# Five of sixteen products per unit on TensorE, and another order of the last steps, in a Mamba and attention/MoE kernel

## The chip, the cores and the metric

One NeuronCore of one Trainium2 chip runs the whole program. The metric is the time of the program on the device in microseconds (us), as the median of several runs.

## The reference, cut to what matters

The input x is 8 sequences of 512 tokens with 128 channels, in float32. Layer one is a Mamba block that runs over each sequence forward and backward, layer two is attention with a mixture of experts. What matters of the first is this:

```python
dt = softplus(dtr @ Wdt.T + bdt)                    # (tokens, 256)
h  = exp(dt_t[..., None] * A) * h + (dt_t * u_t)[..., None] * B_t[:, None, :]   # 16 states for each of 256 channels
y_t = einsum('bdn,bn->bd', h, C_t)
```

The end of layer two adds the two chosen experts' rows of every token to x2, normalizes the sum over its channels, and adds x:

```python
out = out + einsum('tf,hf->th', g, w2[e]) * wfull[:, e:e+1]   # for each expert e
x = x + layernorm(x2 + out)
```

## The kernel before, in words

The first phase (`mamba_phase`) goes through 16 units: for each of the 8 sequences b a forward one (d = 0) and a backward one (d = 1). A unit is 32 steps s, for state n = s // 2 and channel half h = s % 2. Time runs along the free axis (512), channels lie on the partitions. For each step

- ScalarE makes `da` = exp(dt * A) (line 622), up to 8 steps ahead of the scan (`NDA`);
- dt\*u\*B is made in one of two ways. For 12 of the 16 states TensorE spreads B over the partitions into a bank of `bp` (`pe_b`, line 398, one bf16 matmul), and VectorE multiplies by `dtu` into a bank of `dbu` (`dve_dbu`, line 729). For the 4 states in `BY_PE` TensorE makes the whole product, as a matmul of the transposed dt\*u with a diagonal matrix that holds B (`pe_fill`, line 373, four float32 matmuls for each half). The diagonals are made by ScalarE (`act_diag`, line 590, four instructions a state), at the steps in `DIAG_AT`, in two buffers in turn;
- VectorE runs the scan (`dve_scan`, line 745), GpSimd multiplies by C (`pool_hc`, line 874), and TensorE transposes and sums into `yp` (`pe_y`, line 410).

Each engine's order is written out by hand. In `pe_unit` the first fill of a state n is issued at step 2n - 1 and the second at step 2n + 2. Into the same in-order queue go the matmuls that prepare the next unit (`front`): `pe_u` at steps 12 to 18, `pe_z` at 19 and 20 (they wait for ScalarE's silu of u, line 542, which stands behind `da` of step 25), `pe_xd` at 21 (line 339), and `pe_dt` at 24 and 25 (line 389). The previous unit's output (`tail`) is transposed at step 7, copied by ScalarE at its steps 14 and 15 (`act_ygt`, line 630), and, in forward units alone, multiplied by Wout at steps 10 to 13 (`pe_out`, line 432). On VectorE, `dve_dt` makes dt and dtu of the next unit at steps 29 and 30 (lines 715 and 720).

The second phase (`ffn_phase`) runs over slots, 40 for a sequence. A table of due slots (`PLAN`, and `last_plan` for the last three sequences) says at which slot each engine issues a step. At the end of a sequence, SyncE stores the experts' rows (`sp_y`, line 1383), loads x2 again (`sp_x2e`, line 1313, which waits until VectorE has read the former one), and loads x (`sp_xr`); GpSimd gathers each token's two rows (line 2242); VectorE adds them (`ye`, line 2071), takes the statistics (lines 1856 and 1860); and GpSimd normalizes and adds (`pool_rstd`, `pool_out`, lines 2209, 2212 and 2216), and SyncE stores (line 1387). In a slot of SyncE x2e stands ahead of y. VectorE's first `ye` of a sequence waits until `pool_out` of the sequence before is through, because it writes the same tile `ye`.

Of the kernel before, what the change touches and what calls it, by code (L numbers as in the profile page):

```python
# [18 lines left out]
ALU = mybir.AluOpType  # L19
ACT = mybir.ActivationFunctionType  # L20
# [5 lines left out]
P = 128  # L26
NB = 8
# [47 lines left out]
    return isinstance(b, int) and b == 0  # L75


BY_PE = ((2, 4, 12, 14), (2, 4, 6, 14))
N_PE = len(BY_PE[0])
DIAG_AT = ((-1, 5, 18, 20), (-1, 5, 11, 20))  # L80


def made_by_pe(d, n):
# [17 lines left out]
def mamba_phase(nc, sems, x, x1, cscr, w):  # L101

    with ExitStack() as ctx:
# [258 lines left out]
        def pe_fill(pe, b, d, n, h):  # L362

            e = BY_PE[d].index(n)
            if h == 0:
                pe.wait_ge(diag_done, count(diag_done, b, TC * (N_PE * d + e + 1)))
                pe.wait_ge(dtt_done, count(dtt_done, b, 2 * d + 2))
                pe_bank_free(pe, b, d, n)
            else:
                pe.wait_ge(scan_done, count(scan_done, b, STEPS * d + 2 * n - 1))  # L370
            dst = dbu[:, dbu_bank(d, n), :] if h else bp[:, n % 2, :]
            for c in range(TC):
                last = nc.tensor.matmul(dst[:, c * P:(c + 1) * P], dtt[:, c, h * P:(h + 1) * P], diag[:, e % 2, c, :],  # L373
                                        start=True, stop=True)
            last.then_inc(fill_done if h else b_ready, 1)

# [208 lines left out]
        def act_diag(act, b, d, e):  # L585

            act.wait_ge(bt_done, count(bt_done, b, d + 1))
            act.wait_ge(fill_done, count(fill_done, b, N_PE * d + e - 1))
            for c in range(TC):
                nc.scalar.activation(diag[:, e % 2, c, :], ident[:, :], ACT.Copy,  # L590
                                     scale=bt[:, d, c, BY_PE[d][e]:BY_PE[d][e] + 1]).then_inc(diag_done, 1)

        def act_soft(act, b, d, h, k):
# [392 lines left out]
def last_plan(f):  # L986

    if f == NB - 3:
        at = PLAN["down"], PLAN["y_copy"]
        return {"down": at[0][:-1] + (125,), "y_copy": at[1][:-1] + (126,), "y": (99, 109, 119, 126),  # L990
                "gather": (132, 132, 133, 133, 134, 134, 135, 135), "ye": (141, 142),
                "end": (143, 144), "end_rstd": 144, "yo": (144, 145, 146), "out": 147}
    if f == NB - 2:
        return dict(in_pairs(88), w=(73, 80, 80, 97), rows=79, y=(100, 101, 110, 111), x2e=110, xr=110,
                    gather=(114, 114, 115, 115, 116, 116, 117, 117), ye=(129, 130), end=(130, 131), end_rstd=136,
                    yo=(136, 137, 138), out=139)
    if f == NB - 1:
        return dict(in_pairs(68), og_fin=(43, 44, 45, 46), wo=47, post=(48, 49, 49), x2=48, rms=50, h2n=51, x2t=52, h2t=52,
                    gate=54, ex=55, count=57, gate_step=(55,) * 5 + (56,) * 4 + (57,) * 6 + (58,) * 5 + (59,) * 3 + (60,) * 4,
                    scatter=(59, 60, 60, 61, 61, 62, 62, 63), rows=64, w=(61, 62, 69, 70), keep=62, y=(80, 81, 90, 91),  # L1000
                    x2e=91, xr=99, gather=(92, 92, 93, 93, 94, 94, 95, 95), ye=(97, 98), end=(99, 99), end_rstd=100,
                    yo=(100, 101, 102), out=103)
    return {}

# [70 lines left out]
def ffn_phase(nc, sems, x1, out, qscr, kscr, xs, ys, h0s, x2s, w):  # L1075

    with ExitStack() as ctx:
# [776 lines left out]
        def dve_stats(side, src, sem):  # L1854
            for c in range(TC):
                nc.vector.bn_stats(stats[:, side, c, :], src[:, c, :]).then_inc(sem, 1)
# [189 lines left out]
        def dve_g(dve, b, q, f):  # L2046
# [4 lines left out]
            if paired(b):  # L2051
# [5 lines left out]
            nc.vector.scalar_tensor_tensor(g[:, n % 2, 0:w_], ga[:, n % 2, 0:w_], 0.5, bank_of(b, q)[:, 0:w_],  # L2057
                                           ALU.mult, ALU.mult).then_inc(g_done, 1)

        def dve_end(dve, b, k, j=0):  # L2060
            if k == 0:
                if j == 0:
                    dve.wait_ge(gathered, count(gathered, b, 16 * TC * TOP))
                    dve.wait_ge(keep_done, count(keep_done, b, 2))
                    dve.wait_ge(out_done, count(out_done, b, 0))
                    dve.wait_ge(x2e_loaded, count(x2e_loaded, b, 16))
                    dve.wait_ge(end_step, count(end_step, b, 0))
                for c in range(TC):
                    if j:
                        dve.wait_ge(ye_done, count(ye_done, b, c + 1))  # L2070
                    nc.vector.scalar_tensor_tensor(ye[:, c, :], yk[:, c, j, :], wn_e[:, b % 2, c, j:j + 1],  # L2071
                                                   ye[:, c, :] if j else x2e[:, c, :],
                                                   ALU.mult, ALU.add).then_inc(ye_done, 1)
            elif k == 1:
                dve.wait_ge(ye_done, count(ye_done, b, 2 * TC))
                dve_stats(2, ye, end_step)
            else:
                dve_aggr(2, end_step)

        def dve_moe(dve, b, k):  # L2080
# [121 lines left out]
        def pool_out(pool, b, k):  # L2202
# [3 lines left out]
            if k == 0:  # L2206
                pool.wait_ge(end_rstd, count(end_rstd, b, 2))
                pool.wait_ge(out_stored, count(out_stored, b, 0))
                nc.gpsimd.tensor_tensor(yo[:, :, :], ye[:, :, :], mean, ALU.subtract).then_inc(out_done, 1)
            elif k == 1:  # L2210
                pool.wait_ge(out_done, count(out_done, b, 1))
                nc.gpsimd.tensor_tensor(yo[:, :, :], yo[:, :, :], r, ALU.mult).then_inc(out_done, 1)
# [197 lines left out]
```

## Time and profile before

Three runs took 1774.48, 1781.57 and 1783.27 us: a median of 1781.57 us. The profiled execution took 1780.3 us, and its span is 1778.6 us. The first phase ends near 1000 us.

| engine | busy us | share of the span |
|---|---|---|
| VectorE (DVE) | 1386.0 | 78% |
| TensorE (PE) | 1351.9 | 76% |
| GpSimd (POOL) | 1109.5 | 62% |
| ScalarE (ACT) | 1063.5 | 60% |

A share of busy time is a mean over the two phases. The row of busy tenths in 40 slices shows VectorE at nine tenths or more in every slice of the first phase after its start, and at four to eight tenths in most of the second. The granted TensorE clock is 0.88 of full speed over the span.

### The profile page before, as it was taken

What the parts mean: (1) busy time and instruction counts of PE and PEld (TensorE: products, weight loads), DVE (VectorE), ACT (ScalarE), POOL (GpSimd) and SP (SyncE); (2) the same over time, 40 slices, a digit from 0 to 9 for tenths busy, and PEclk for the clock granted to TensorE, in tenths of its full rate; (3) what the DMA queues carried; (4) which work ended last, traced back from release to release, by engine and by line L of the source; (5) the groups of instructions that cost most, each with busy time, mean ns of one, the idle gap of its engine ahead of it and who ended that gap; (6) DMA issues with size and microseconds to landing.
All of it is one profiled execution on the core that took longest, in us unless ns stands there. A gap on an engine that the chain in (4) does not pass through costs nothing. (4 is left out here: it accounts for less than half of the span.)

```text
span 1778.6 us, 30876 instructions
## 1 busy us (share of the span) xinstructions
PE 1351.9 (76%) x8880; PEld 980.9 (55%) x8880; DVE 1386.0 (78%) x2234; ACT 1063.5 (60%) x1888; POOL 1109.5 (62%) x1244
## 2 busy tenths in 40 slices
PE   3877787678777877887786427888989889888671
PEld 1566566556655665666565413335665566656571
DVE  1999999999899999999999416677678777777422
ACT  4777677776776776867766023655555555556330
POOL 1677777777777777877777423445456466555535
PEclk9898999898899898998897658888899998999886
DMA  4122302320223023202220111134556455454662
GB/s 133 55 101 96 120 1 95 119 95 18 102 95 119 1 95 119 95 17 103 95 95 19 31 51 46 44 97 130 164 170 200 143 170 159 131 186 153 216 209 69
DMA packets 114410, 184.90 MB, mean 104 GB/s; under 512 B 10384, under 2 KB 87184, under 8 KB 109968
## 3 DMA queue, kind: packets, MB, share of 16 engines
q1 hardware_dynamic: 110192, 175.15, 28.7%
q0 software_dynamic: 4096, 8.40, 1.6%
q8 instruction: 44, 0.72, 0.2%
q14 instruction: 78, 0.64, 0.1%
HBM read 153.03 MB, written 25.89 MB: 101 GB/s over the span
## 5 line engine op out<-in xcount | busy, mean ns | idle before, releaser
L874 POOL TENSOR_TENSOR hc<-hb,cb 128x512 f32<-128x512 f32 x512 | 653.6, 1296 | 208.4 <-DVE hb L745 178.1
L745 DVE TENSOR_TENSOR_SCAN hb<-da,dbu 128x512 f32<-128x512 f32 x448 | 527.7, 1205 | 19.0 <-PE dbu L373 13.3
L622 ACT ACTIVATE da<-dt,a_neg 128x512 f32<-128x512 f32 x512 | 351.7, 716 | 188.9 <-DVE hb L745 160.5
L410 PE MATMUL yp<-ident,hc 128*128 128x128 f32 x2048 | 327.0, 295 | 3.2 <-POOL hc L874 3.1
L410 PEld LDWEIGHTS yp<-ident,hc 128*128 128x128 f32 x2048 | 278.0, 155 | 83.0 <-issue 54.9
L1764 ACT ACTIVATE pt<-scores,lift 128x512 f32<-128x512 f32 x320 | 216.4, 684 | 169.7 <-PE scores L1515 161.9
L1891 DVE TENSOR_REDUCE mx<-ms 128x1 f32<-128x384 f32 (+3 forms) x352 | 218.3, 636 | 117.7 <-PE ms L1477 111.2
L729 DVE TENSOR_TENSOR dbu<-dtu,bp 128x512 f32<-128x512 f32 x384 | 251.3, 684 | 16.5 <-PE bp L398 7.3
L2222 POOL TENSOR_SCALAR_AFFINE_SELECT pt<-pt 128x256 f32<-128x256 f32 (+1 forms) x320 | 119.0, 375 | 199.0 <-ACT pt L1764 197.0
L321 PE MATMUL wp<-xpad,wu 128*128 128x512 f32 x256 | 132.1, 608 | 11.4 <-DVE res L760 6.5
L1477 PE MATMUL ms<-k,q 72*128 72x384 bf16 (+3 forms) x512 | 136.8, 326 | 0.0
L1515 PE MATMUL scores<-q,k 75*128 75x384 bf16 (+3 forms) x512 | 131.2, 319 | 2.2 <-ACT pt L1764 2.1
L1474 PE MATMUL ms<-mask,identb 128*128 128x128 bf16 (+2 forms) x352 | 92.2, 262 | 52.9 <-DVE mx L1891 23.1
L1534 PE MATMUL og<-pt,vpad 128*32 128x512 f32 (+3 forms) x1024 | 98.8, 484 | 23.4 <-POOL pt L2222 23.2
L2242 POOL DMA_INDIRECT yk<-ys_scratch,pos_e x64 | 61.6, 962 | 50.7 <-DMA ys_scratch<-ysb 35.8
L359 PE MATMUL wp<-ident,dtu 128*128 128x128 f32 x128 | 31.5, 427 | 80.0 <-DVE dtu L720 80.0
L398 PE MATMUL bp<-st,sel 96*128 96x512 bf16 x192 | 79.5, 414 | 11.9 <-DVE dbu L729 9.3
L1515 PEld LDWEIGHTS scores<-q,k 75*128 75x128 bf16 x512 | 48.9, 103 | 64.6 <-issue 34.6
L1474 PEld LDWEIGHTS ms<-mask,identb 128*128 128x128 bf16 x352 | 36.2, 103 | 87.5 <-issue 42.9
L373 PE MATMUL dbu<-diag,dtt 128*128 128x128 f32 x512 | 70.9, 282 | 15.6 <-DVE hb L745 15.1
L590 ACT ACTIVATE diag<-ident,bt 128x128 f32<-128x128 f32 x256 | 81.2, 389 | 1.6
L373 PEld LDWEIGHTS dbu<-diag,dtt 128*128 128x128 f32 x512 | 63.8, 192 | 31.6 <-DVE hb L745 24.9
(228 smaller groups left out, 2441.7 us busy)
## 6 DMA issues: line engine op xcount, KB each, us to landing
cb<-c_scratch SPq DMA_DIRECT2D x16, 3072.0 KB, 11.6
wt<-ffn_w_e SPq DMA_DIRECT2D x120, 384.0 KB, 4.3
cb<-c_scratch SPq DMA_DIRECT2D x16, 1024.0 KB, 4.5
q<-q_scratch SPq DMA_DIRECT2D x96, 96.0 KB
xg<-xs_scratch SPq DMA_DIRECT2D x24, 256.0 KB, 3.4
ys_scratch<-ysb SPq DMA_DIRECT2D x24, 256.0 KB
q_scratch<-qp SPq DMA_DIRECT2D x24, 128.0 KB
k<-k_scratch SPq DMA_DIRECT2D x32, 72.0 KB
```

What stands on the lines that cost most here:

```text
L321: last = nc.tensor.matmul(wp[:, h, :], wu[:, d, j, h * P:(h + 1) * P], xpad[:, d, j:j + SEQ], start=(j == 0), stop=(j == NTAP - 1))
L373: last = nc.tensor.matmul(dst[:, c * P:(c + 1) * P], dtt[:, c, h * P:(h + 1) * P], diag[:, e % 2, c, :], start=True, stop=True)
L410: last = nc.tensor.matmul(yp[:, c, h * P:(h + 1) * P], src[:, c * P:(c + 1) * P], ident[:, :], is_transpose=True, start=(s < 0 and h == 0 ...
L622: nc.scalar.activation(da[:, s % NDA, :], dt[:, h, :], ACT.Exp, scale=a_neg[:, d, h, n:n + 1]).then_inc(da_done, 1)
L729: nc.vector.tensor_tensor(dbu[:, dbu_bank(d, n) ^ h, :], dtu[:, h, :], bp[:, n % 2, :], ALU.mult).then_inc(dbu_done, 1)
L745: nc.vector.tensor_tensor_scan(hb[:, s % NHB, :], da[:, s % NDA, :], src, 0.0, ALU.mult, ALU.add).then_inc(scan_done, 1)
L874: nc.gpsimd.tensor_tensor(hc[:, s % NHC, :], hb[:, s % NHB, :], cb[:, d, s // 2, :], ALU.mult).then_inc(hc_done, 1)
L1474: nc.tensor.matmul(heads[:, :, c * P:width], identb[:, :], mask[:, :].unsqueeze(1).to_broadcast([P, n, P]), start=True, stop=False, skip_g ...
L1477: last = nc.tensor.matmul(heads[:, i, :], q9[0:PART_ROWS, at, h0_ % GH + i, c * P:(c + 1) * P], k9[0:PART_ROWS, at, 0:width], start=False, ...
L1515: last = nc.tensor.matmul(sp_[:, t % 2, at:at + SEQ - kc * P], k9[:, group, kc * P:(kc + 1) * P], q9[:, group, h % GH, kc * P:], start=Tru ...
L1764: nc.scalar.activation(pt[:, (ST_TILES * b + t) % NPR, 0:width], scores_in, ACT.Exp, bias=lift[:, :], scale=SCALE).then_inc(exp_done, 1)
L1891: nc.vector.reduce_max(mx[:, c, h:h + n], ms[:, t % 2, 0:n * (c + 1) * P].rearrange("p (n k) -> p n k", n=n), mybir.AxisListType.X).then_i ...
```

## The change

1. `BY_PE` has five states: (2, 4, 10, 12, 14) in forward units and (2, 4, 6, 12, 14) in backward ones. So state 10 is added in forward units and state 12 in backward ones, and their diagonals at ScalarE's steps 14 and 18; the forward unit's diagonal of state 14 moves from step 20 to step 28. With an odd number in a unit, the buffer of a diagonal goes by the count over both units.
2. In the last sequence, `x2e` is due one slot later (92, not 91), behind the last `y` of slot 91.
3. In the last sequence, `ye` is written into the tile `x2e` in place. The wait for GpSimd's `pool_out` of the sequence before goes from the first addition to the aggregation of the statistics, which writes the means that `pool_out` reads.

```diff
-BY_PE = ((2, 4, 12, 14), (2, 4, 6, 14))
+BY_PE = ((2, 4, 10, 12, 14), (2, 4, 6, 12, 14))
 N_PE = len(BY_PE[0])
-DIAG_AT = ((-1, 5, 18, 20), (-1, 5, 11, 20))
+DIAG_AT = ((-1, 5, 14, 18, 28), (-1, 5, 11, 18, 20))
...
-                last = nc.tensor.matmul(dst[:, c * P:(c + 1) * P], dtt[:, c, h * P:(h + 1) * P], diag[:, e % 2, c, :],
+                last = nc.tensor.matmul(dst[:, c * P:(c + 1) * P], dtt[:, c, h * P:(h + 1) * P], diag[:, (N_PE * d + e) % 2, c, :],
...
-                nc.scalar.activation(diag[:, e % 2, c, :], ident[:, :], ACT.Copy,
+                nc.scalar.activation(diag[:, (N_PE * d + e) % 2, c, :], ident[:, :], ACT.Copy,
...
-                    x2e=91, xr=99, gather=(92, 92, 93, 93, 94, 94, 95, 95), ye=(97, 98), end=(99, 99), end_rstd=100,
+                    x2e=92, xr=99, gather=(92, 92, 93, 93, 94, 94, 95, 95), ye=(97, 98), end=(99, 99), end_rstd=100,
...
+        def ye_of(b):
+
+            return x2e if b == NB - 1 else ye
+
...
-                    dve.wait_ge(out_done, count(out_done, b, 0))
+                    if b < NB - 1:
+                        dve.wait_ge(out_done, count(out_done, b, 0))
...
-                    nc.vector.scalar_tensor_tensor(ye[:, c, :], yk[:, c, j, :], wn_e[:, b % 2, c, j:j + 1],
-                                                   ye[:, c, :] if j else x2e[:, c, :],
+                    nc.vector.scalar_tensor_tensor(ye_of(b)[:, c, :], yk[:, c, j, :], wn_e[:, b % 2, c, j:j + 1],
+                                                   ye_of(b)[:, c, :] if j else x2e[:, c, :],
...
-                dve_stats(2, ye, end_step)
-            else:
+                dve_stats(2, ye_of(b), end_step)
+            else:
+                if b == NB - 1:
+                    dve.wait_ge(out_done, count(out_done, b, 0))
                 dve_aggr(2, end_step)
...
-                nc.gpsimd.tensor_tensor(yo[:, :, :], ye[:, :, :], mean, ALU.subtract).then_inc(out_done, 1)
+                nc.gpsimd.tensor_tensor(yo[:, :, :], ye_of(b)[:, :, :], mean, ALU.subtract).then_inc(out_done, 1)
```

## Rows read from the trace of the kernel before

**Rows 1.** Groups of instructions by line: busy us, mean ns, idle before.

```profile
L729 DVE TENSOR_TENSOR dbu<-dtu,bp 128x512 f32<-128x512 f32 x384 | 251.3, 684 | 16.5 <-PE bp L398 7.3 <-DVE hb L745 0.9
```

**Rows 2.** Busy time by stretch, two forward units, a backward unit, stretch after a wait.

```profile
283.20:343.00 59.80, 46.99 (x300) 36.86 (x299) 58.63 (x73) 41.39 (x75) 45.84 (x38) 0.93 0.23 89
402.60:464.40 61.80, 49.73 (x298) 38.81 (x297) 58.12 (x73) 41.28 (x74) 45.72 (x38) 0.89 0.22 86
...
464.40:522.20 57.80, 45.10 (x269) 35.10 (x268) 56.19 (x68) 45.57 (x84) 45.18 (x40) 0.91 0.18 73
...
436.50:444.50 8.00, 8.00 (x25) 5.76 (x26) 8.00 (x12) 4.42 (x7) 6.39 (x6) 0.62 0.29 98
```

**Rows 3.** VectorE in a forward unit by start time, and all instructions of L715.

```profile
318.95 1.26 DVE L729 TENSOR_TENSOR dbu<-dtu,bp 128x512 f32<-128x512 f32 x2
320.12 2.32 DVE L745 TENSOR_TENSOR_SCAN hb<-da,dbu 128x512 f32<-128x512 f32 x2
...
325.78 1.19 DVE L745 TENSOR_TENSOR_SCAN hb<-da,bp 128x512 f32<-128x512 f32 x1
...
331.78 1.19 DVE L745 TENSOR_TENSOR_SCAN hb<-da,bp 128x512 f32<-128x512 f32 x1
...
L715 DVE TENSOR_TENSOR dt<-t_ln,t_relu x16: 1224/1910/2589, 43.6 to 935.6; 128x1024 f32<-128x1024 f32 x16
```

**Rows 4.** TensorE in the same forward unit, by start time.

```profile
317.13 1.13 PE L330 MATMUL wp<-win_z,xpad 128*128 128x256 f32 x4 [2.81 <-ACT u L542]
...
321.78 0.60 PE L410 MATMUL yp<-ident,hc 128*128 128x128 f32 x4
322.21 1.06 PE L373 MATMUL bp<-diag,dtt 128*128 128x128 f32 x8
```

**Rows 5.** TensorE and VectorE in a backward unit, by start time.

```profile
504.66 1.12 PE L389 MATMUL wp<-xd,wdt 128*128 128x512 f32 x2 [0.39 <-ACT xd L563]
...
507.14 0.60 PE L410 MATMUL yp<-ident,hc 128*128 128x128 f32 x4
...
509.88 2.32 DVE L745 TENSOR_TENSOR_SCAN hb<-da,dbu 128x512 f32<-128x512 f32 x2
```

**Rows 6.** The same, in a backward and a forward unit with TensorE at half clock.

```profile
388.50 0.60 PE L410 MATMUL yp<-ident,hc 128*128 128x128 f32 x4
...
390.02 2.33 DVE L745 TENSOR_TENSOR_SCAN hb<-da,dbu 128x512 f32<-128x512 f32 x2
...
444.09 0.60 PE L410 MATMUL yp<-ident,hc 128*128 128x128 f32 x4
...
449.92 1.22 DVE L745 TENSOR_TENSOR_SCAN hb<-da,dbu 128x512 f32<-128x512 f32 x1 [1.65 <-PE dbu L373]
```

**Rows 7.** TensorE's first product with Wout, and ScalarE's diagonals, in a forward unit.

```profile
297.36 1.16 PE L432 MATMUL wp<-wout,ygt 128*128 128x128 f32 x8 [0.59 <-ACT ygt L630]
...
301.61 1.26 ACT L590 ACTIVATE diag<-ident,bt 128x128 f32<-128x128 f32 x4
```

**Rows 8.** The last 33 us by start time, and what SyncE waited for there.

```profile
1745.84 1.54 SPq L1383 DMA_DIRECT2D ys_scratch<-ysb  x3
1748.06 0.36 SPq L1313 DMA_DIRECT2D x2e<-x_scratch  x1
1748.52 0.54 SPq L1383 DMA_DIRECT2D ys_scratch<-ysb  x1
...
1752.56 0.94 POOL L2242 DMA_INDIRECT yk<-ys_scratch,pos_e  x1 [8.34 <-DMA ys_scratch<-ysb]
...
1765.91 1.26 POOL L2216 TENSOR_TENSOR yo<-yo,xr 128x512 f32<-128x512 f32 x1
...
1767.36 1.14 DVE L2071 SCALAR_TENSOR_TENSOR ye<-yk,wn_e,x2e 128x128 f32<-128x128 f32 x4 [18.05 <-POOL yo L2216]
...
1772.33 1.04 POOL L2209 TENSOR_TENSOR yo<-ye,mv 128x512 f32<-128x512 f32 x1
...
SPq L1077 <- DMA out<-yo: 1.9, 1, 1.9
```

## The prediction

> **What bounds the kernel now.** I read the busy tenths first, then the groups by line, then single units by their start times, and last the chain of waits at the end.
>
> In the first phase VectorE is the engine that never rests: in a forward unit of 59.8 us it is busy 58.6 us, TensorE 47.0, GpSimd 45.8, ScalarE 41.4 [rows 2]. The multiplication that the change takes away costs 684 ns each, and VectorE waited 16.5 us in all for what feeds it [rows 1]. So by shares VectorE is the bound, and one multiplication less should be one multiplication of time. But TensorE works through one hand-written order, and a share does not say whether a fill is ready when the scan asks for it. So the reader is to look at TensorE's start times beside VectorE's.
>
> Two things stand out. TensorE sits idle 2.81 us before the z matmuls of the next unit (it waits for ScalarE's silu), and from there on it works without a pause: z, y, xd, fills, dt [rows 4]. And forward units come in two lengths, 59.8 and 61.8 us [rows 2]: in the longer one that chain runs at a granted clock of 0.62, part of it at 1.2 and not at 2.4 GHz, and the scan waits 1.65 us for a fill [rows 2, 6]. I count this half clock behind the z wait in five of the eight forward units and in four of the seven backward units that prepare another; there the wait is 2.2 us.
>
> In the last 33 us the end is a chain over engines: store, gather, GpSimd's output of the sequence before, VectorE's additions, GpSimd's output, store [rows 8].
>
> **Part 1: the nominal gain.** Two multiplications go, a pair taking 1.17 us from start to next start (318.95 to 320.12). But the next state's multiplications then stand between the two scans. Four scans with one pair of multiplications took 5.66 us in one piece (320.12 to 325.78) and 6.00 us when interleaved (325.78 to 331.78), 0.34 more [rows 3]. So a state moved to TensorE gives 1.17 - 0.34 = 0.83 us, in 16 units 13.3 us, if its data are there in time.
>
> **Part 2: is the fill there in time, forward?** State 10's second fill is issued at step 22, which is just behind xd, where the y group starts at 321.78 now. A fill takes 1.06 us [rows 4], and I add 0.19 for the signal (the gap that I read wherever a scan waited for one): scan 21 can start at 323.03. Nominally it would start at 320.12 - 1.17 + 1.9 = 320.85, so it is 2.2 us late. Nothing upstream moves: the z wait ends 4.0 us after scan 17 starts, and scan 17 lies ahead of the change. Then come scan 21 with the multiplication behind it (1.85) and two scans (2.24): scan 24 starts at 327.12 instead of 325.78 [rows 3], +1.34. The second fill of state 12 is pushed back by the added 0.9 us and just makes it. Of the 1.34, dt gives back some: it took 2.59 us there, against a median of 1.91 [rows 3], because GpSimd was behind. That lag vanishes when the scans come later; I give back 0.7. A full-clock forward unit: +0.6 us, three of them +1.9.
>
> With the half clock: y behind xd starts at 444.09, so scan 21 at 445.34, scan 24 at 449.43, scan 25 at 451.33 instead of 449.92 [rows 6]: +1.4, five units +7.0.
>
> **Part 3: backward.** State 12's second fill is issued at step 26, behind both dt matmuls, where y starts at 507.14 now. Its first fill, at step 23, takes the place of a bf16 matmul and costs 0.67 more, of which TensorE's wait of 0.39 before dt hides its part: +0.28 [rows 5]. Scan 25 can start at 507.14 + 0.28 + 1.25 = 508.67, scan 26 at 510.52 instead of 509.88 [rows 5]: +0.64, three units +1.9. With the half clock: 388.50 + 0.28 + 1.25 + 1.85 = 391.88 instead of 390.02 [rows 6]: +1.86, four units +7.4. The last backward unit prepares nothing, so its TensorE queue is free: -0.8.
>
> Bounds for one added state: -0.83 (fill in time) and +1.9. I take the middle values above because each comes from the queue order and a start time.
>
> **Part 4: the diagonals.** Four more instructions, 1.26 us a unit on ScalarE [rows 7], which is idle 18 of 60 us [rows 2]. At step 18 in backward units and at step 28 in forward ones they fall into waits: nothing. At step 14 in forward units they stand ahead of the two copies `ygt` for which TensorE already waits 0.59 us [rows 7]. The product with Wout starts some 1.2 us later; the scans' data are 4 us ahead there, and TensorE waits 0.9 us again a little later for VectorE's `res`. What remains, 0.2 to 0.3, comes off the z wait. If that cover were gone it would cost up to 1.2 us a forward unit.
>
> **Part 5: the clock.** In forward units the z wait shrinks from 2.81 by 0.67 (the first fill of state 10 goes into it) and by those 0.23, to 1.9 us. Waits of 2.8 were followed by the half clock five times of eight and waits of 2.2 four times of seven, so 1.9 should be followed by it less often. A half-clock forward unit is 63.2 us by my sums and a full one 60.4, 2.8 to 2.9 between. The first unit's wait is longer (4.2) and keeps it. Bounds: none of the other four changes (0), or all do (-11.5). I take three: -8.7. The Trainium skill ("TensorE: Matmul & The Clock Gate", the part on the HAM clock gate) says that the array falls to half its clock after idling and gets it back by sustained work. By it all forward units but the first might stay at 2.4 GHz, a rival below; the rows of before agree that the low clock stands behind waits, and show no wait as short as 1.9.
>
> **Part 6: the end.** The last store of expert rows waits behind x2e on SyncE's queue: the three before it are issued by 1747.38, x2e waits for VectorE until 1748.06, the fourth goes at 1748.52 [rows 8]. With x2e behind it, the store is 1.1 us earlier, and so is the gather (1752.56) and what GpSimd does behind it: its third `yo` ends at 1766.1, not 1767.17. The additions then no longer wait for that. If they are done by then, only the aggregation and the root follow (4.97 us from 1767.36 to 1772.33, less 3.1 for additions and statistics: 1.9), and `yo` starts at 1768.0, 4.3 earlier. What is late next is the store of the sequence before, which reads `yo`: issued 0.5 after 1766.1, and SyncE waited 1.9 us after issuing such a store [rows 8], so it lands near 1769.0: -3.3. Bounds: -1.1 (the additions run only after `yo`) and -4.3. I take -3.0. The Trainium skill ("SBUF — State Buffer", "Who interferes with whom") says that a VectorE instruction with two SBUF inputs and a GpSimd instruction that reads SBUF block each other for the whole instruction. By it the additions would be strung between the three `yo`, and the end gains nearer 2 than 3. The spread of dt, 1.22 to 2.59 us for one shape [rows 3], agrees with it.
>
> **The sum.** 1.9 + 7.0 + 1.9 + 7.4 - 0.8 = +17.4; clock -8.7; end -3.0: +5.7 us on the profiled execution's 1780.3, so 1786.0. That execution lies 1.3 us under the median of the three runs (1781.57), within their spread of 9 us.
>
> **The rivals.**
> A. The fills are in time and VectorE is the bound: -13.3 - 3.0, 1764. For it: VectorE's 98% share in a unit. Against it: the start times of rows 4 and 5, and that a fill is waited for already [rows 6].
> B. The half clock stays as often as it was, or comes more often, because the longer work moves the waits about: +17.4 - 3.0, 1795, slower than before. Its place is the chain behind the z wait, its price 2.9 us a forward unit; it decides once at most one of the four forward units gets its clock back. For it: backward waits stay 2.2 us. Against it: Part 5.
> C. The half clock disappears behind all z waits but the first: another -2.9, and four backward units at (1.86 - 0.64) + 0.4 (what that clock costs them now) = 1.6 each, -6.5: 1777.
>
> **How the numbers follow.** Chances: forecast 0.45, A 0.20, B 0.20, C 0.15. What three runs of this kernel can tell from no change is about 0.5%, so the borders are 1772.7 and 1790.5. Faster: 0.18 of A, 0.03 of the forecast, 0.04 of C, 0.25 in all. Slower: 0.19 of B and 0.11 of the forecast, 0.30. Same: 0.45. The forecast's own range is 1776 to 1795 (the bounds of the clock and of the end); to hold 8 in 10 it must reach A and B: 1764 to 1799.
>
> **What would show it.** Line 729 falls from 384 to 352 instructions. If I am right, in forward units scan 21 starts 0.2 us after a fill ends, about 9.9 us after scan 17, and in backward units scan 25 does, 14.7 us after scan 17 at full clock; VectorE's idle time before line 745, ended by TensorE's line 373, grows from some 16 us to over 40; the z wait of forward units is near 1.9 us. Wrong: scan 21 starts 1.9 us after scan 20 with the fill long ready (then A), or units whose lengths differ by 2 us or more in another share than I took (B or C). At the end the additions should start while GpSimd writes `yo` of the sequence before, and the last `yo` should start some 6 us after that `yo` began, not 8.6.

## The result, and the profile after

The changed kernel took 1791.95 us (median of 9 runs, 1782.71 to 1799.12), the kernel before 1779.36 us (9 runs, 1767.01 to 1783.27): a ratio of 1.0089, with an interval of 1.0061 to 1.0117. The forecast was 1786.0: 6 us under the median. The profiled execution took 1785.23 us (span 1783.5), 0.8 under the forecast, but it was the second shortest of the nine, with the highest granted clock (0.899, down to 0.881 in the others). So that agreement is partly luck. The likeliest case was a change within 0.5%; by the ratio the kernel is slower, by 0.9%, as the rival B had it. (The ratios here and below are estimates from the undisturbed executions of both kernels, without one of 7195.6 us in experiment 3, so they differ a little from the quotients of the medians, 1.0071 here.) The steps have to be looked at one by one.

The groups by line first (line, operation, count, busy us, mean ns, idle before and its largest releaser). After, they answer to [rows 1]:

```profile
L745 DVE TENSOR_TENSOR_SCAN hb<-da,dbu 128x512 f32<-128x512 f32 x432 | 510.0, 1206 | 36.4 <-POOL hc L874 17.0
...
L729 DVE TENSOR_TENSOR dbu<-dtu,bp 128x512 f32<-128x512 f32 x352 | 233.1, 687 | 19.7 <-PE bp L398 7.9
...
L373 PE MATMUL dbu<-diag,dtt 128*128 128x128 f32 x640 | 88.3, 281 | 17.3 <-DVE hb L745 17.3
```

The 32 multiplications are gone (384 to 352, 251.3 to 233.1 us), and the scans wait 36.4 us; on the page of before that was 19.0. VectorE lost 18 us of work and gained as much waiting.

Next, busy time by stretch (length; then PE, PEld, DVE, ACT and POOL busy, PEclk, DMA share, GB/s): the whole first phase, from the first scan to the end of the last; a forward unit at full clock; one with half clock behind the z wait; a backward unit without and one with it; and, of the forward unit with half clock, the 8 us around it. They answer to [rows 2].

```profile
47.44:999.39 951.95, 747.34 (x4659) 590.90 (x4657) 895.37 (x1055) 692.65 (x1274) 718.55 (x597) 0.92 0.19 76
287.67:348.64 60.97, 47.94 (x314) 38.18 (x313) 57.78 (x72) 42.53 (x78) 45.78 (x38) 0.95 0.22 87
527.22:590.11 62.89, 49.55 (x315) 39.51 (x314) 57.78 (x71) 42.84 (x79) 45.85 (x38) 0.91 0.22 85
348.64:406.83 58.19, 46.47 (x284) 36.78 (x283) 55.33 (x67) 46.66 (x88) 45.21 (x40) 0.91 0.17 73
228.25:287.67 59.42, 47.21 (x284) 36.56 (x283) 55.45 (x66) 46.63 (x88) 45.17 (x40) 0.90 0.18 72
...
560.50:568.50 8.00, 7.35 (x31) 5.50 (x32) 4.35 (x8) 5.61 (x9) 5.50 (x5) 0.79 0.28 98
```

Before, the same stretch:

```profile
47.28:993.35 946.07, 743.52 (x4419) 581.33 (x4417) 907.75 (x1087) 674.82 (x1210) 718.36 (x597) 0.89 0.19 77
```

So the first phase is 5.9 us longer, at a clock of 0.92 instead of 0.89. Forward units at full clock, 59.6 to 59.8 us long before, now take 60.7 to 61.2, and VectorE is busy 0.9 us less in each. Half clock behind the z wait follows in 3 of 8 forward and 4 of 7 backward units; before it was 5 and 4.

Now the fill of state 10 in a full-clock forward unit, by start time (start, us, engine and line, [idle before and releaser]); scan 17 starts at 317.61 there. TensorE, answering to [rows 4], then VectorE, answering to [rows 3]:

```profile
321.61 1.13 PE L330 MATMUL wp<-win_z,xpad 128*128 128x256 f32 x4 [2.14 <-ACT u L542]
...
324.53 1.88 PE L339 MATMUL wp<-u,wx 128*128 128x512 f32 x4
326.25 1.05 PE L373 MATMUL dbu<-diag,dtt 128*128 128x128 f32 x8
```

```profile
324.71 0.70 DVE L729 TENSOR_TENSOR dbu<-dtu,bp 128x512 f32<-128x512 f32 x1
327.50 1.22 DVE L745 TENSOR_TENSOR_SCAN hb<-da,dbu 128x512 f32<-128x512 f32 x1 [2.09 <-POOL hc L874]
```

The fill stands behind xd, ends at 327.30, and scan 21 starts 0.2 later, 9.89 us after scan 17 (forecast 9.9). The profile puts the wait down to GpSimd's `hc`. Experiment 2 shows that it was the fill. The same is seen in the other units: in 14 of the 15 that prepare another, scan 21 (forward) or 25 (backward) starts 0.19 us after its fill ends, whichever of the two engines the profile names. Together these waits come to about 29 us (17.0 put down to `hc` and 12.1 to the fills of line 373), where the forecast had over 40.

A backward unit at full clock, answering to [rows 5]: the fill of state 12 behind both dt matmuls, and the scan that waits for it.

```profile
391.33 1.05 PE L373 MATMUL dbu<-diag,dtt 128*128 128x128 f32 x8
```

```profile
392.58 1.22 DVE L745 TENSOR_TENSOR_SCAN hb<-da,dbu 128x512 f32<-128x512 f32 x1 [1.12 <-PE dbu L373]
```

Scan 25 starts 14.48 us after scan 17 (378.10; forecast 14.7).

The end, by start time, answering to [rows 8]:

```profile
1752.49 2.31 SPq L1383 DMA_DIRECT2D ys_scratch<-ysb  x4
...
1754.89 0.78 SPq L1313 DMA_DIRECT2D x2e<-x_scratch  x1
...
1758.40 0.94 POOL L2249 DMA_INDIRECT yk<-ys_scratch,pos_e  x1 [7.52 <-DMA ys_scratch<-ysb]
...
1769.52 1.03 POOL L2216 TENSOR_TENSOR yo<-ye,mv 128x512 f32<-128x512 f32 x1
1769.70 4.77 DVE L2076 SCALAR_TENSOR_TENSOR x2e<-yk,wn_e,x2e 128x128 f32<-128x128 f32 x8 [13.74 <-DMA yk<-ys_scratch,pos_e]
...
1771.75 1.26 POOL L2223 TENSOR_TENSOR yo<-yo,xr 128x512 f32<-128x512 f32 x1
...
1777.26 1.04 POOL L2216 TENSOR_TENSOR yo<-x2e,mv 128x512 f32<-128x512 f32 x1
```

All four stores go together ahead of x2e, and the additions run beside GpSimd's `yo`, which is three instructions for a sequence. From the start of the third `yo` of the sequence before to the first of the last one it is 5.51 us; it was 6.42 [rows 8]. From the first of the three it is 7.74 us; it was 8.65 (1763.68 to 1772.33). Of the eight additions the first three took 1.00, 1.19 and 1.42 us, and each ended 0.15 us after one of the three `yo`; the other five, with GpSimd idle, took 0.34 us each.

### The profile page after: what moved, and what is told of

Its sections match the earlier page's. It is cut to its first block and busy times, and to the rows that moved or that the text cites. A ratio compares the mean times of both kernels' runs of the same rounds, so it can differ in the third digit from the quotient of the medians.

```text
span 1783.5 us, 31398 instructions
## 1 busy us (share of the span) xinstructions
PE 1347.0 (76%) x9120; PEld 984.9 (55%) x9120; DVE 1375.8 (77%) x2202; ACT 1081.3 (61%) x1952; POOL 1109.3 (62%) x1244
## 5 line engine op out<-in xcount | busy, mean ns | idle before, releaser
L745 DVE TENSOR_TENSOR_SCAN hb<-da,dbu 128x512 f32<-128x512 f32 x432 | 510.0, 1206 | 36.4 <-POOL hc L874 17.0
L410 PE MATMUL yp<-ident,hc 128*128 128x128 f32 x2048 | 319.1, 290 | 3.5 <-POOL hc L874 3.3
L410 PEld LDWEIGHTS yp<-ident,hc 128*128 128x128 f32 x2048 | 268.9, 152 | 70.8 <-issue 42.1
L729 DVE TENSOR_TENSOR dbu<-dtu,bp 128x512 f32<-128x512 f32 x352 | 233.1, 687 | 19.7 <-PE bp L398 7.9
L1474 PE MATMUL ms<-mask,identb 128*128 128x128 bf16 (+2 forms) x352 | 91.2, 259 | 59.6 <-DVE mx L1891 27.2
L373 PEld LDWEIGHTS dbu<-diag,dtt 128*128 128x128 f32 x640 | 80.7, 192 | 41.7 <-DVE hb L745 27.9
L590 ACT ACTIVATE diag<-ident,bt 128x128 f32<-128x128 f32 x320 | 101.5, 389 | 2.6 <-PE dbu L373 0.8
L373 PE MATMUL dbu<-diag,dtt 128*128 128x128 f32 x640 | 88.3, 281 | 17.3 <-DVE hb L745 17.3
L745 DVE TENSOR_TENSOR_SCAN hb<-da,bp 128x512 f32<-128x512 f32 x80 | 95.8, 1198 | 0.5
L2249 POOL DMA_INDIRECT yk<-ys_scratch,pos_e x64 | 61.8, 966 | 53.3 <-DMA ys_scratch<-ysb 38.5
L373 PE MATMUL bp<-diag,dtt 128*128 128x128 f32 x640 | 88.0, 282 | 4.6 <-issue 1.9
```

Source lines behind the costliest of these rows:

```text
L410: last = nc.tensor.matmul(yp[:, c, h * P:(h + 1) * P], src[:, c * P:(c + 1) * P], ident[:, :], is_transpose=True, start=(s < 0 and h == 0 ...
L729: nc.vector.tensor_tensor(dbu[:, dbu_bank(d, n) ^ h, :], dtu[:, h, :], bp[:, n % 2, :], ALU.mult).then_inc(dbu_done, 1)
L745: nc.vector.tensor_tensor_scan(hb[:, s % NHB, :], da[:, s % NDA, :], src, 0.0, ALU.mult, ALU.add).then_inc(scan_done, 1)
L1474: nc.tensor.matmul(heads[:, :, c * P:width], identb[:, :], mask[:, :].unsqueeze(1).to_broadcast([P, n, P]), start=True, stop=False, skip_g ...
```

## The experiments

Each ratio is to the kernel before, timed beside it on the same chip. The chips differ: the kernel before took 1780.45 us beside the kernels of experiment 1, the first of 2 and the first of 3, 1765.19 us beside the others of 2 and 3 and the first of 4, and 1764.04 us beside the rest. So times from different chips are compared by their ratios, and an expectation in microseconds has to be read as a ratio too. "First phase" is the stretch from the first scan to the end of the last, in the profiled execution.

**1. The two halves of the change by themselves.** One kernel has the change in the units without that of the end, one the reverse.

```diff
 # units alone, against the kernel before (cut: a diagonal's buffer as in the change)
-BY_PE = ((2, 4, 12, 14), (2, 4, 6, 14))
+BY_PE = ((2, 4, 10, 12, 14), (2, 4, 6, 12, 14))
-DIAG_AT = ((-1, 5, 18, 20), (-1, 5, 11, 20))
+DIAG_AT = ((-1, 5, 14, 18, 28), (-1, 5, 11, 18, 20))
```

```diff
 # end alone, against the changed kernel
-BY_PE = ((2, 4, 10, 12, 14), (2, 4, 6, 12, 14))
+BY_PE = ((2, 4, 12, 14), (2, 4, 6, 14))
-DIAG_AT = ((-1, 5, 14, 18, 28), (-1, 5, 11, 18, 20))
+DIAG_AT = ((-1, 5, 18, 20), (-1, 5, 11, 20))
```

> The change of the units alone (five states, the diagonals), with the end of the program as before. Theory (late fills): the whole slowdown is here; against the kernel before +13 to +16 us, and scan 21 of full-clock forward units 9.9 us after scan 17, as in the changed kernel. Rival (the end of the program turned against it): the same time as before, within 4 us.

> The end alone, with the four states a unit of before. Theory: -1 to -2 us against before (0.8 from the store that no longer stands behind x2e, 0.9 from the additions, which lose most of their lead to the overlap with GpSimd's yo), so a ratio of 0.999, hardly to be told from 1. My prediction had -3.0. Rival (the end gains all of its 4.3, or costs something): 0.9975, or above 1.001.

Units alone: 1792.68 us, ratio 1.0075 (1.0045 to 1.0104). The end alone: 1773.32 us, 0.9975 (0.9936 to 1.0014), which by time alone tells nothing from zero. Its middle is just the figure that the expectation gave to the rival, the end gaining all of its 4.3 us, but the interval holds both. The whole slowdown is that of the units; the sign and the size of the end's gain rest on the start times, which repeat those of the changed kernel (the gather starts 8.50 us after the last gather of the sequence before; 8.46 in the changed kernel, 9.28 before; and from the first `yo` of the sequence before to that of the last it is 7.73 us).

The second kernel has the units of the kernel before, instruction by instruction, and its first phase is 14 us shorter than the one profiled before (931.7, not 946.1):

```profile
48.56:980.22 931.66, 729.14 (x4419) 569.99 (x4417) 906.56 (x1087) 674.18 (x1210) 718.42 (x597) 0.90 0.19 78
```

It had half clock behind the z wait in 4 forward and 3 backward units, and in the forward ones it lasted 3.4 us, not 6.8 (6.0 of them behind the start of z). So two profiles differ by such amounts without any change in the program, and the 5.9 us between the profiled pair say little by themselves. The units with five states were profiled twice more, unchanged: 952.1 us in the kernel with the units alone, 956.1 us in that of experiment 5. Against 946.1 and 931.7 us with four states, the execution profiled before was a long one.

**2. The fill ahead of what it stood behind.** In the changed kernel, the second fill of state 10 goes ahead of the second half of z, and that of state 12 ahead of dt, with the matmuls for B that belong to the next scan; in a second kernel the same turn is made with the four states of before. The lines that take them out of their old places are cut here.

```diff
+                    if s == 20 and 10 in FILL_EARLY[d]:
+                        pe_fill(pe, b, d, 10, 1)     # four states: not this one
+                        pe_b(pe, b, d, 11)
...
+                    if s == 24:
+                        pe_b(pe, b, d, 13)
+                        pe_fill(pe, b, d, 12, 1)
```

> The changed kernel with TensorE's order altered and nothing else: in units that prepare another, state 10's second fill and the spread of B for state 11 go ahead of the second z matmul (forward), and the spread for state 13 and state 12's second fill go ahead of the first dt matmul (both kinds). The same instructions in all. Theory (the slowdown is the place of the second fills in TensorE's queue): scan 21 follows scan 20 after 1.9 us, scan 17 to scan 22 takes 9.6 us and not 11.75 in full-clock forward units, scan 17 to 26 takes 15.1 in backward ones and not 16.3; forward units near 59.3, backward ones near 57.2, the time 1762 to 1772. Rival 1 (a state on TensorE is worth nothing whatever its place, for instance because GpSimd's products or the handing over between engines eat it): stays within 5 us of the changed kernel. Rival 2 (pushing z and dt back makes the next unit's dt late): the scans are in time, but the time from scan 29 to the next unit grows by 1 us or more, and the total is that of the changed kernel or worse.

> The kernel before (four states, its own end of the program) with the same turn in TensorE's order as the run with early fills: the spread of B for state 11 ahead of the second z matmul in forward units, that for state 13 ahead of the first dt matmul in both kinds, and state 12's second fill there too in forward units. It tells whether the gain of that run is the order alone. Theory (fifth state worth 0.8 us a unit once its fill is in time): full-clock forward units stay at 59.7 and backward ones at 57.8, since nothing waited there; only half-clock forward units gain, some 1.5 us each; 3 to 8 us under before, and the early-fills kernel stays 8 us or more ahead. Rival (the fifth state is worth nothing, the order is all): as fast as the early-fills kernel, 0.992 of before.

Five states: 1764.75 us, 0.992 (0.9882 to 0.9957). Four states: 1758.41 us, 0.9964 (0.9936 to 0.9992). The intervals overlap, so the times alone do not show the fifth state ahead; they show that the late place was the slowdown. With four states and this order, half clock stood behind z in 11 of 15 units, and yet the forward units behind the first took 59.4 to 60.4 us: half clock costs little where no scan waits for a fill behind it. In the five-state kernel, a full-clock forward unit (scan 17 at 307.68), TensorE and VectorE:

```profile
311.68 1.13 PE L332 MATMUL wp<-win_z,xpad 128*128 128x256 f32 x4 [2.14 <-ACT u L550]
...
313.08 1.06 PE L375 MATMUL dbu<-diag,dtt 128*128 128x128 f32 x8
```

```profile
314.79 0.70 DVE L737 TENSOR_TENSOR dbu<-dtu,bp 128x512 f32<-128x512 f32 x1
315.39 1.21 DVE L753 TENSOR_TENSOR_SCAN hb<-da,dbu 128x512 f32<-128x512 f32 x1
```

Scan 21 starts 7.71 us after scan 17, and waits for nothing. Nothing on GpSimd was changed, so the 2.09 us put down to `hc` were the wait for the fill. From scan 17 to scan 26 it is 15.56 us (17.75 in the changed kernel, 16.40 before), and 15.11 in backward units (16.34, 15.95). So the fifth state is worth 0.84 us up to that scan in either kind, the nominal gain of Part 1 (0.83), if its fill is there (at full clock). But the stretch from scan 29 to the next unit took 8.93 us in backward units, where the changed kernel has 8.24. That is experiment 4's question.

**3. TensorE's wait ahead of z filled with matmuls.** In the first kernel, all four matmuls of the last `pe_u` group are done twice; in the other two, only two more stand ahead of that group, whose results it overwrites; they are put into the changed kernel and into the kernel before.

```diff
 # four more, in the changed kernel
+            for j in range(NTAP if i == NH2 * NTAP - 1 else 0):
+                last = nc.tensor.matmul(wp[:, h, :], wu[...j...], xpad[...], start=(j == 0), stop=(j == NTAP - 1))
```

```diff
 # two more, in the changed kernel and in that of before
+            for m in range(2 if i == NTAP else 0):
+                nc.tensor.matmul(wp[:, h, :], wu[...m...], xpad[...], start=(m == 0), stop=(m == 1))
```

> The changed kernel with the four matmuls of the second channel half of u done twice, so that TensorE works 1.7 us more in the wait before z (2.15 us now, then 0.4). The output is the same. Theory (late fills at full clock, and half clock on top in about half of the units): no unit but the first has the half clock behind z any more; forward units 61.0, backward ones 58.2, the total 5 to 12 us below the changed kernel and still 2 to 6 above before. Rival (the clock is the whole slowdown): at or below the time before. Rival (the clock behind z does not matter, the added work does): 10 us or more above the changed kernel.

> The changed kernel with two u matmuls of 0.86 us done once more (their result is overwritten by the group behind them, the output is the same), so that the wait before z shrinks from 2.15 to about 0.4 us and z is not pushed back. Theory (late fills cost at full clock; half clock on top): no half clock behind z but perhaps in the first unit; forward units 60.9, backward 58.2, z still 4.0 us after scan 17; time 1783 to 1788, less than the changed kernel and still above before. Rival (the slowdown is clock alone): 1776 or less.

> The kernel before with the same two extra matmuls; the wait before z shrinks from 2.8 to 1.1 us in forward units and from 2.15 to 0.4 in backward ones. Theory: the half clock behind z, which costs the kernel before about 2 us in a forward unit and 0.5 in a backward one where it falls, goes: forward 59.7, backward 57.8 in all units, 6 to 12 us under before, and the changed kernel with the same matmuls is 10 us or more behind this one. Rival (the half clock behind z costs nothing that is seen in the total): same as before.

Four more were too many: 1799.22 us, 1.0108 (1.0062 to 1.0153), where 5 to 12 us under the changed kernel were expected. The half clock behind z was gone in all units, but the repeated matmuls take 3.6 us (1.7 expected), more than the wait had, and z starts 5.12 us after scan 17 (318.58), not 4.00; everything behind it is late by that:

```profile
318.95 3.60 PE L324 MATMUL wp<-xpad,wu 128*128 128x512 f32 x8
...
323.71 1.03 PE L333 MATMUL wp<-win_z,xpad 128*128 128x256 f32 x4
```

With two more the wait is 1.1 us in forward units of the kernel before and 0.43 in those of the changed one, and z starts where it did. The kernel before became 1753.39 us, 0.9937 (0.9907 to 0.9966), the changed one 1772.73 us, 1.0043 (1.0014 to 1.0071). That is under the 1776 us of the rival "clock alone", but on a chip on which the kernel before took 1765.19; by the ratio the changed kernel is still slower than before, and 19 us behind the filled kernel of before, so the rival is out. The first phase and the rest of the kernel before, and of the changed kernel, both filled:

```profile
50.18:976.87 926.69, 743.27 (x4479) 572.59 (x4477) 907.87 (x1087) 674.43 (x1210) 718.99 (x597) 0.92 0.20 78
976.87:1748.30 771.43, 578.11 (x4416) 380.37 (x4416) 470.31 (x1134) 365.13 (x638) 387.32 (x634) 0.87 0.44 137
```

```profile
50.30:994.17 943.87, 768.26 (x4719) 602.03 (x4717) 894.74 (x1055) 692.98 (x1274) 719.14 (x597) 0.92 0.20 77
994.17:1775.40 781.23, 594.84 (x4416) 389.31 (x4416) 474.23 (x1135) 365.84 (x638) 386.71 (x634) 0.85 0.44 135
```

At one clock, 0.92, the change costs 17.2 us in the first phase. Unit against unit without any half clock it is 1.34 us in each forward unit (59.7 to 61.0) and 0.40 in each backward one (16.34 against 15.95 from scan 17 to 26), less 0.8 in the last: 8 x 1.34 + 7 x 0.40 - 0.8 = 12.7. The other 4.5 are half clock left in the filled changed kernel, behind z in the first unit and ahead of it in two backward ones. The late fills are therefore structural, and the clock is a second effect on top. (The second phase, which is the same but for the end, differs by 9.8 us at 0.87 and 0.85; over all the profiles, what lies outside the first phase takes 820 to 843 us: another reason to read single stretches.)

**4. Fills early and wait filled; then VectorE's dt kept clear of GpSimd.** The first kernel has the edits of 2 and the two matmuls of 3; it was timed twice. In the next, GpSimd is held at step 29 until dt is done; in the last, that hold alone is put into the changed kernel.

```diff
+                if front and s == 29:
+                    pool.wait_ge(dt_done, count(dt_done, front[0], 2 * front[1] + 1))
```

> Early fills and the two extra matmuls together. Theory: forward 59.0, backward 57.2, no half clock behind z; since the early-fills profile had it in only three of fifteen units, at most 3 us better than that kernel: 1760 to 1766. Rival (more work on TensorE now pushes something that the early order had just in time): worse than the early-fills kernel by 3 us or more.

> The kernel with early fills and the two extra matmuls once more, to have it on one chip with the next one: 0.990 to 0.994 of before, backward units 57.2 with 8.9 us from scan 29 to the next unit (8.2 in the kernel before) and a dt instruction of 2.6 us.

> Early fills, the two extra matmuls, and GpSimd waits before its product of step 29 until the next unit's dt is made. Theory (what the fifth state gained at scan 26, 0.84 us in each kind, is given back at dt, which has both inputs in SBUF and waits while GpSimd's products are behind): dt takes 1.2 to 1.5 us and not 2.6, scan 29 to the next unit falls from 8.9 to some 7.8 us in backward units and from 9.4 to some 8.3 in forward ones, 12 to 16 us under the same kernel without the wait. Rival (dt is long by itself when the scans come sooner, or waits for ScalarE's t_ln): dt stays at 2 us or more, nothing gained. Rival (GpSimd, held back by 1 us, is late for the next unit's scans): dt short, but the first eight scans take longer by as much.

> The changed kernel with that wait of GpSimd alone. In my prediction I gave back 0.7 us at dt in full-clock forward units, and the trace of the changed kernel shows 2.58 us for dt there, as before. Theory: dt falls to 1.2 to 1.5 us, scan 29 to the next unit from 9.1 to 8.0 in forward units and from 8.2 to 7.7 in backward ones, scan 17 to 21 stays 9.9; 8 to 14 us under the changed kernel, so about the time of before. Rival (GpSimd is not what dt waits for): no change.

Without the hold: 1748.47 us, 0.9916 (0.9883 to 0.995), and again 1749.9 us, 0.993 (0.9904 to 0.9956). The first phase is 921.7 us, only 5.0 less than the 926.7 of four states with the wait filled, where 0.84 a unit would give 13. The next two fences show the same place of a backward unit, VectorE and GpSimd, without the hold and with it:

```profile
504.47 0.69 DVE L740 TENSOR_TENSOR dbu<-dtu,bp 128x512 f32<-128x512 f32 x1
505.07 2.59 DVE L726 TENSOR_TENSOR dt<-t_ln,t_relu 128x1024 f32<-128x1024 f32 x1
...
501.63 4.95 POOL L885 TENSOR_TENSOR hc<-hb,cb 128x512 f32<-128x512 f32 x4
508.95 2.09 POOL L885 TENSOR_TENSOR hc<-hb,cb 128x512 f32<-128x512 f32 x1 [2.38 <-DVE hb L756]
```

```profile
500.49 1.35 DVE L726 TENSOR_TENSOR dt<-t_ln,t_relu 128x1024 f32<-128x1024 f32 x1
501.76 1.21 DVE L756 TENSOR_TENSOR_SCAN hb<-da,dbu 128x512 f32<-128x512 f32 x1
502.89 1.53 DVE L731 TENSOR_TENSOR dtu<-dt,u 128x1024 f32<-128x1024 f32 x1
...
497.03 3.72 POOL L885 TENSOR_TENSOR hc<-hb,cb 128x512 f32<-128x512 f32 x3
502.07 3.48 POOL L885 TENSOR_TENSOR hc<-hb,cb 128x512 f32<-128x512 f32 x2 [1.32 <-DVE dt L726]
```

Without it dt "takes" 2.59 us, and ends about 1.1 after GpSimd's fourth `hc` (506.58): its time holds a wait of some 1.2 us for GpSimd. With it dt takes 1.35, and dtu (1.53) 0.34 more than its 1.19. By all sixteen of each (ns, minimum, median and maximum; without and with the hold):

```profile
L726 DVE TENSOR_TENSOR dt<-t_ln,t_relu x16: 1226/2586/2598, 44.9 to 912.3; 128x1024 f32<-128x1024 f32 x16
```

```profile
L726 DVE TENSOR_TENSOR dt<-t_ln,t_relu x16: 1226/1352/1373, 44.5 to 904.5; 128x1024 f32<-128x1024 f32 x16
```

The time is 1739.85 us (1736.17 to 1743.08), 0.9876 (0.9835 to 0.9917): the fastest version, ahead of both kernels, though 10 us under the same kernel without the hold and not the expected 12 to 16. Its first phase is 913.1 us, 8.4 less than without the hold. 6.0 of them are in backward units (scan 29 to the next unit 8.93 to 8.02 us), 2.2 in forward ones, most of it in the first and the last; in the others that stretch stays at 8.9 to 9.6 us with dt short. There VectorE now sits idle 1.01 us before the first multiplication of the next unit (0.29 without the hold); what it waits for was not tried. Nor was the hold tried with four states, whose dt in forward units is 2.6 us long as well, so how much of the 8.4 us belongs to the fifth state stays open. In the changed kernel, the hold gave 1767.1 us, 1.0024 (0.999 to 1.0058), not told from no change, against 1.0089 for the change without it: forward units gained (scan 29 to the next unit 9.14 to 8.00), but six of seven backward units had the half clock there, and their sum was 415.2 us (412.2 in the changed kernel).

**5. The end with the additions kept clear of GpSimd.** GpSimd's first `yo` of the sequence before waits until the additions of the last are done.

```diff
+                if b == NB - 2:
+                    pool.wait_ge(ye_done, count(ye_done, NB - 1, 2 * TC))
```

> The changed kernel with GpSimd's first yo of the last sequence but one held until the last sequence's eight additions are made, so that they do not run side by side. Theory (both read two tiles of SBUF, and they hold each other up): the eight additions take 2.2 us and not 4.8; the last yo starts within 1 us of where it does now, counted from the last gather. Rival (the additions are slow because they write x2e in place): they still take over 4 us.

One execution, of 1790.89 us; there is no ratio. The end by start time:

```profile
1773.09 2.19 DVE L2076 SCALAR_TENSOR_TENSOR x2e<-yk,wn_e,x2e 128x128 f32<-128x128 f32 x8 [13.70 <-DMA yk<-ys_scratch,pos_e]
...
1775.45 1.04 POOL L2218 TENSOR_TENSOR yo<-ye,mv 128x512 f32<-128x512 f32 x1 [2.60 <-DVE x2e L2076]
...
1779.05 0.38 DVE L1860 BATCH_NORM_AGGREGATE mv<-stats 128x2 f32<-128x6 f32 x4 [2.86 <-POOL yo L2225]
...
1782.89 1.04 POOL L2218 TENSOR_TENSOR yo<-x2e,mv 128x512 f32<-128x512 f32 x1 [2.08 <-DMA out<-yo]
```

The eight additions took 2.19 us, 4.77 beside GpSimd. So their length in the changed kernel was GpSimd's doing. But from the first gather of the last sequence to the end it is 27.30 us, not 25.09: the aggregation waits 2.86 us for `yo`, and then the last `yo` 2.08 us for the store of the one before, the wait that Part 6 named as next. The hold pushed both back. Within 1 us either way was the wrong expectation; it costs 2.2.

## Why the prediction was right, and where it was not

**What bounds, and Part 2's mechanism: right.** VectorE was the bound by shares and the order of TensorE's queue decided. Scan 21 came 9.89 us after scan 17, for 9.9, and scan 26 1.35 us later than before (17.75 against 16.40), for 1.34; moved ahead of the second half of z and of xd, it was in time at full clock (experiment 2). But VectorE's waits for fills came to 29 us, not to over 40.

**Part 2, the 0.7 given back at dt: wrong.** This is the step that failed, "that lag vanishes when the scans come later". At full clock dt took 2.58 us, for 2.59, and GpSimd began the product of step 29 0.87 us after the scan, for 0.89 before, so nothing came back. I had moved the scans and not the rest: GpSimd's `rem` and `st` for the next unit wait for xd, which stands in the same late queue, so they came later together with the scans (14.4 and 19.2 us behind scan 17, for 13.0 and 17.8). That this is why is read from start times; that GpSimd makes dt long is shown by experiment 4. A full-clock forward unit thus costs 1.2 to 1.34, not 0.6.

**Part 2, half clock: a little dear, and by other terms.** A half-clock forward unit behind the first is 62.8 us, for 61.8 before: +1.0, not 1.4. From scan 17 to scan 26 only 0.1 was added (19.42 for 19.3), because the half clock lasted 3.4 us and not 6.8; against units of before with 3.4 (18.01, in the end-alone kernel) it is the 1.4 that I had. The rest is dt again, which in the half-clock unit of before (1.91 us) ran beside GpSimd for part of its time only, and then for all of it. Before and after:

```profile
696.67 1.91 DVE L715 TENSOR_TENSOR dt<-t_ln,t_relu 128x1024 f32<-128x1024 f32 x1
```

```profile
568.71 1.22 DVE L745 TENSOR_TENSOR_SCAN hb<-da,dbu 128x512 f32<-128x512 f32 x1 [2.95 <-PE dbu L373]
...
582.57 2.58 DVE L715 TENSOR_TENSOR dt<-t_ln,t_relu 128x1024 f32<-128x1024 f32 x1
```

**Part 3: right up to scan 26, wrong for whole units.** From scan 17 to scan 26 the late fill cost 0.39 us at full clock, for 0.64, and 1.6 at half clock (18.01 against 16.41), for 1.86; the last unit gained 0.84, for 0.8. But the seven backward units that prepare another, and the last, grew by 1.3 us together, not by 8.5. Three units of before had another half clock, some 27 us ahead of z and 6.8 us long, which came in no unit after. The way from the unit's start to scan 17 is 30.6 us with it, 29.5 where it lasts 3.4 us, and 29.0 without. These are such a stretch and one with 3.4 us, before:

```profile
343.04:373.62 30.58, 26.61 (x161) 21.52 (x160) 28.00 (x38) 22.21 (x44) 22.39 (x21) 0.88 0.00 0
464.45:493.93 29.48, 26.13 (x162) 21.00 (x161) 28.01 (x38) 22.25 (x45) 22.45 (x22) 0.91 0.00 0
```

Over the seven units, the shorter way to scan 17 gave 4.8 us. No term of the prediction is about it, and by experiment 1 it comes and goes without a change of program.

**Part 4: right.** From the start of a full-clock forward unit to scan 17 it is 29.94 us in both kernels (283.20 to 313.14, and 287.67 to 317.61), so the diagonals cost nothing. They did not take 0.2 off the z wait either: it fell from 2.81 to 2.14, which is the fill's 0.67 alone, not to 1.9.

**Part 5: right in direction, wrong in price and reason.** Half clock behind z fell from five forward units to three (I took three fewer; it was two: three lost it and one gained it), and it was shorter. A forward unit with it is 1.8 us longer than one without (62.8 against 61.0), not 2.8 to 2.9. The reason was misread as well: the first unit's wait was 4.2 us, so waits of 2.8 were followed by half clock in four of seven units, just as those of 2.2 were, and the rows of before gave no ground for "less often" at 1.9. With five states, waits of 2.14 were followed by it in two, two and three of seven forward units of the three profiles; with four, those of 2.81 in four and three of seven.

**The sum: a balance of misses.** The first phase of the profiled pair came to +5.9, where my terms say 17.4 - 8.7 = +8.7. Taken apart, the near agreement is luck. The forward units grew by 4.5 us, not by 1.9 + 7.0 - 8.7 = 0.2, and 3.5 of that lie behind scan 29, where I had given time back. The backward units grew by 1.3, not by 8.5. Against the 12.7 us of experiment 3, the clock gave back 6.8 in this pair, and hid the missing give-back at dt. The medians differ by 12.6, and experiment 1 shows why one pair can't settle this term. How much half clock a typical execution of either kernel has stays open. The range has a slip too: the bounds of the clock and of the end that it names give 1782 to 1797, not 1776 to 1795.

**Part 6: right in mechanism, too large.** The stores were released as forecast: the gather came 0.8 us sooner (1.1 expected). The last `yo` started 7.7 us after the first of the three before it, for 6 (8.6 before the change), and the end as a whole, both stretches together, gained 0.8 + 0.9 = 1.7 us, not 3.0. What was mis-sized is the additions' time: I had them done by the end of `yo` (1766.1 in the forecast's count), but they took 4.77 us beside GpSimd and ended 1.5 us behind the third `yo` (1774.47 against 1773.01). Beside the forecast I had a rule of the Trainium skill ("SBUF — State Buffer", "Who interferes with whom"): a VectorE instruction with two SBUF inputs and a GpSimd instruction that reads SBUF exclude each other for a whole instruction. The traces agree: one addition was made for each `yo` (1.00, 1.19 and 1.42 us, and 0.34 for each of the rest), the eight took 4.77 us beside GpSimd and 2.19 without it, dt 2.59 and 1.35. By that rule I had written that the end gains nearer 2 than 3, and it was 1.7.

**The rivals.** A (fills in time) is refuted for this kernel, and its price too: with fills made to be in time, at one clock, the units gained not 13.3 us but 5.0, since dt gave most of it back, until GpSimd was held. B (half clock as often as before, 1795, or 1.0083 of the profiled execution before) was not the profiled execution's way, where the half clock shrank; but its size is that of the measured ratio, 1.0089, as the late fills cost more than I had and the clock gave part of it back. C (half clock gone, 1777, or 0.998) was brought about in experiment 3, and even then the ratio is 1.0043.

## What to carry to other kernels

Work taken off a saturated engine pays only if the replacement is ready: write down where in the other engine's in-order queue it is issued and what stands ahead of it, and if it comes late, move it before judging the idea (here 1.0089 for the change became 0.992 with the fills moved, and 0.9876 with two more repairs, of which the hold was not tried on the kernel before). Where a later event is to "give back" time, look whether the work that causes the contention moves along with it; it did here. And when an engine's clock varies between executions of one program, compare unit with unit at one clock, or fill the waits in both kernels, before calling a difference of spans an effect.

## What was not expected of the hardware

- Two matmuls whose result nobody reads, in a wait of 2.8 us (2.2 in backward units), made the kernel before 0.6% faster (0.9937): half clock behind z went from 9 of 15 units to none. Waits of 1.1 us were followed by it in no unit, those of 2.1 to 2.2 us in some units and not in others, and in other units from one execution to the next.
- The gain of removing VectorE's 684 ns was 0.84 us a state at scan 26, and 0.3 us a unit at the end of the unit (5.0 us of 16 units, TensorE's wait filled in both), while VectorE and GpSimd met at one instruction, dt: 1.35 us when GpSimd was held back, 2.59 when not.
- The profile named GpSimd's `hc` for 17.0 of the 36.4 us for which the scans waited. It was the other wait of the same instruction, TensorE's fill, which ended 0.2 us before the scan began in all nine of these waits.
